# Layer 1 of a sparse graph attention kernel: the owner mask made with ScalarE, owners weighted on ScalarE, score products in smaller pieces

## What is computed

```
h = relu(layernorm(x)); x = x + elu(softmax_adj(leaky_relu(h W a1 + (h W a2)^T)) @ (h W))
h = relu(layernorm(x))
q, k, v = h Wq^T + bq, h Wk^T + bk, h Wv^T + bv
scores  = where(adj > 0, q k^T / sqrt(128), -9e15)
x = x + elu(softmax(scores) @ v)
```

## Time and profile before

| | before |
|---|---|
| median of 3 runs | 1752.17 us (1751.08 to 1753.33) |
| span of the profiled execution | 1752.0 us |
| first and last gather of layer 1 start | 961.48 and 1728.84 us |
| VectorE busy | 1346.6 us (77%), 5825 instructions |
| TensorE busy | 1194.1 us (68%) |
| GpSimd busy | 1175.3 us (67%), 1206 instructions |
| ScalarE busy | 779.5 us (44%) |
| DMA in layer 1 | about 60 GB/s, near 390 GB/s in layer 0 |

### The profile page before, as it was taken

One profiled execution on the slowest core, in us unless ns is written; L12 is line 12 of the kernel. 1 busy time (PEld: TensorE's weight loads), 2 busy tenths in 40 slices (PEclk: granted clock), 3 DMA queues, 4 the chain that ended last, 5 costly groups with the idle time before them and its releaser, 6 DMA issues.

```text
span 1752.0 us, 21963 instructions
## 1 busy us (share of the span) xinstructions
PE 1194.1 (68%) x5314; PEld 931.3 (53%) x5362; DVE 1346.6 (77%) x5825; ACT 779.5 (44%) x1507; POOL 1175.3 (67%) x1206
## 2 busy tenths in 40 slices
PE   2667785867677677776763577677676676766675
PEld 1444453545454455454553566666666666666664
DVE  3468996989888889888896577777767777777776
ACT  2768776877777777877722111111111111111111
POOL 1227775776666676666674777777777777777773
PEclk9778777777777777777755555655656656666665
DMA  9869999999999999999722222222222222222221
GB/s 292 336 245 389 395 396 400 393 391 382 368 381 378 378 393 388 385 376 386 272 64 55 53 56 62 62 60 61 55 60 62 59 62 62 61 62 60 63 62 38
DMA packets 122254, 372.34 MB, mean 213 GB/s; under 512 B 34577, under 2 KB 67858, under 8 KB 89362
## 3 DMA queue, kind: packets, MB, share of 16 engines
q1 hardware_dynamic: 75458, 289.83, 43.1%
q0 software_dynamic: 38464, 81.08, 17.0%
q10 hardware_dynamic: 8208, 0.03, 0.3%
HBM read 358.12 MB, written 12.72 MB: 212 GB/s over the span
## 4 chain that ended last, share of the span: by engine, by line
POOL 35%; DVE 20%; DMA 14%; issue 13%; PE 9%; ACT 5%; SPq 2%; POOLq 0%; ACTq 0%; DVEq 0%
POOL arena L603 34%; DMA table<-arena 12%; ACT arena L1173 4%; PE psum L1412 4%; PE psum L1398 3%; POOL arena L573 2%; DMA arena<-in_adj_dram 1%; DVE arena L759 1%; DVE arena L792 1%; DVE arena L874 1%; DVE arena L867 1%; DVE arena L762 1%; PE psum L1384 1%; DVE arena L883 1%; SPq L446 1%
## 5 line engine op out<-in xcount | busy, mean ns | idle before, releaser
L573 POOL DMA_INDIRECT arena<-table,arena x576 | 553.9, 962 | 266.4 <-issue 159.5
L603 POOL DMA_INDIRECT arena<-table,arena x576 | 593.1, 1030 | 184.0 <-issue 175.2
L1173 ACT ACTIVATE arena<-arena 128x2048 bf16<-128x2048 int32 x256 | 484.9, 1895 | 32.7 <-DMA arena<-in_adj_dram 32.5
L1384 PE MATMUL psum<-arena 128*128 128x18 f32 x768 | 138.7, 312 | 277.2 <-DVE arena L840 277.1
L1351 PE MATMUL psum<-arena 128*128 128x512 bf16 x976 | 291.9, 447 | 24.6 <-ACT arena L1173 20.6
L1384 PEld LDWEIGHTS psum<-arena 128*128 128x128 f32 x768 | 125.2, 242 | 309.5 <-DVE arena L840 309.5
L874 DVE SCALAR_TENSOR_TENSOR arena<-arena 128x131 f32<-128x131 f32 (+1 forms) x768 | 267.7, 349 | 15.4
L1398 PE MATMUL psum<-arena 128*128 128x131 f32 (+1 forms) x768 | 200.9, 433 | 93.5 <-DVE arena L867 93.5
L1398 PEld LDWEIGHTS psum<-arena 128*128 128x128 f32 x768 | 179.3, 329 | 97.2 <-issue 97.2
L1121 DVE TENSOR_TENSOR arena<-arena 128x903 f32<-128x903 f32 x64 | 70.5, 1101 | 177.7 <-DMA arena<-table,arena 177.7
L1351 PEld LDWEIGHTS psum<-arena 128*128 128x128 bf16 x1024 | 117.4, 120 | 164.0 <-issue 84.9
(11 more groups left out here) (199 smaller groups left out, 1993.3 us busy)
## 6 DMA issues: line engine op xcount, KB each, us to landing
arena<-in_adj_dram SPq DMA_DIRECT2D x256, 1024.0 KB, 15.5
arena<-table,arena POOLq DMA_INDIRECT x1152
table<-arena POOLq DMA_DIRECT2D x32, 132.0 KB, 5.0
arena<-table SPq DMA_DIRECT2D x64, 66.0 KB, 15.1
table<-arena SPq DMA_DIRECT2D x16, 256.0 KB, 15.2
arena<-table SPq DMA_DIRECT2D x64, 64.0 KB, 2.1
out_dram<-arena SPq DMA_DIRECT2D x16, 256.0 KB, 2.4
arena<-in_x_dram SPq DMA_DIRECT2D x4, 0.5 KB, 12.3
```

The lines of the kernel that those rows point to most:

```text
L573: pool.indirect_dma_start(Gt[:, v % GROUP, c + 1, :], None, table0, bass.IndirectOffsetOnAxis(idx_now[:, v % GROUP, c:c + 1], 0))\
L603: pool.indirect_dma_start(Gt[:, t % GROUP, c + 1, 0:D], None, table1, bass.IndirectOffsetOnAxis(idx_now[:, t % GROUP, c:c + 1], 0))\
L1173: nc.scalar.activation(mask[:, k, q * QUARTER:(q + 1) * QUARTER], adj_sb[:, k, q, :], ACT.Relu, accum_out=sum_all[:, bass.ds(tile, 1), q:q ...
L1384: last = nc.tensor.matmul(by_slot_ps[k], owned[:, r, c, :], slot_e[:, k, c, :], start=(c == 0), stop=(c == CHUNKS - 1))
```

## The change

`from_end` and the two-step mask are gone. Before the loop VectorE makes three constants: `iota_odd` = 2 x place + 1 (float16), `mid_all` = -(pre + end) and `len_all` = end - pre. ScalarE writes `dist` = |iota_odd + mid| in float16, two buffers, one tile ahead. VectorE makes the mask with one compare, dist < len. The owners are weighted on ScalarE with three activations of 128 columns, right after the exponential, one step earlier than before in the order of the lists; in the place where `weigh` stood VectorE now waits for the first exponential only, ahead of the add-slots. The score products are written in pieces: own slots two at a time (2, 2, 2, 1), owner slots one at a time (3). The sum over them (L1127) is as before.

```
@@ prepare
-                    dve.wait_ge(mine_done, T + t)
-                    nc.vector.tensor_scalar(from_end[:, :], iota16[:, :], end_all[:, at], None, ALU.is_ge).then_inc(fe_done, 1)
...
-                    dve.wait_ge(fe_done, T + t + 1)
-                    nc.vector.scalar_tensor_tensor(out=mine[:, b, :], in0=iota16[:, :], scalar=pre_all[:, at],
-                                                   in1=from_end[:, :], op0=ALU.is_ge, op1=ALU.subtract).then_inc(mine_done, 1)
+                    dve.wait_ge(dist_done, t + 1)
+                    nc.vector.tensor_scalar(mine[:, b, :], dist[:, b % 2, :], len_all[:, at], None, ALU.is_lt)\
+                      .then_inc(mine_done, 1)
@@ score1
-                    nc.vector.tensor_tensor(prod[:, 0:OWN, :], Gt[:, b, 0:OWN, 0:DE],
-                                            u_row[:, b:b + 1, P:].to_broadcast([P, OWN, DE]), ALU.mult).then_inc(e_done, 1)
+                    for c in range(0, OWN, 2):
+                        end = min(c + 2, OWN)
+                        nc.vector.tensor_tensor(prod[:, c:end, :], Gt[:, b, c:end, 0:DE],
+                                                u_row[:, b:b + 1, P:].to_broadcast([P, end - c, DE]), ALU.mult)\
+                          .then_inc(e_done, 1)
                     dve.wait_ge(own_done, u + 1)
-                    nc.vector.tensor_tensor(prod[:, OWN:ROWS, :], Gt[:, b, OWN:ROWS, 0:DE], uq_ps[k], ALU.mult)\
-                      .then_inc(e_done, 1)
-                    dve.wait_ge(e_done, T + 2 * u + 2)
+                    for c in range(CHUNKS):
+                        nc.vector.tensor_tensor(prod[:, OWN + c, :], Gt[:, b, OWN + c, 0:DE], uq_ps[k][:, c, :], ALU.mult)\
+                          .then_inc(e_done, 1)
+                    dve.wait_ge(e_done, T + PRODUCTS * (u + 1))
@@ attend, VectorE
-                        if live(t, 3):
-                            weigh(T + t - 3, m, back)
...
                         if live(t, 3):
+                            dve.wait_ge(p_done, 2 * (T + t - 3) + 1)
                             for c in range(OWN):
@@ before the loop, VectorE
+                nc.vector.tensor_scalar(iota_odd[:, :], iota16[:, :], 2.0, 1.0, ALU.mult, ALU.add).then_inc(spans_done, 1)
+                nc.vector.scalar_tensor_tensor(out=mid_all[:, :], in0=pre_all[:, :], scalar=-1.0, in1=end_all[:, :],
+                                               op0=ALU.mult, op1=ALU.subtract).then_inc(spans_done, 1)
+                nc.vector.tensor_tensor(len_all[:, :], end_all[:, :], pre_all[:, :], ALU.subtract).then_inc(spans_done, 1)
@@ ScalarE
+                def measure_spans(t):
+                    nc.scalar.activation(dist[:, t % 2, :], iota_odd[:, :], ACT.Abs, bias=mid_all[:, t:t + 1]).then_inc(dist_done, 1)
+
+                def weigh_owners(tt, k, r):
+                    act.wait_ge(p_done, 2 * tt + 2)
+                    act.wait_ge(owned_done, tt + 1)
+                    act.wait_ge(acc_done, tt)
+                    for c in range(CHUNKS):
+                        last = nc.scalar.activation(weighted[:, c, :], owned[:, r, c, :], ACT.Identity,
+                                                    scale=p10[:, k, OWN + c:OWN + c + 1])
+                    last.then_inc(weighted_done, 1)
...
+                        if live(t, -1):
+                            if t >= 1:
+                                act.wait_ge(mine_done, T + t)
+                            measure_spans(t + 1)
                         if live(t, 4):
...
                         if live(t, 2):
                             prob_over(T + t - 2, k)
+                            weigh_owners(T + t - 2, k, (b - 2) % GROUP)
```

More of the change, by code:

```diff
@@ L214, in two_layer_graph_attention @@
         accT = place([2, P])
+        iota_odd = place([QCOLS], F16)
+        dist = place([2, QCOLS], F16)
+        mid_all = place([T])
+        len_all = place([T])
         top[0] = common
@@ L347, in two_layer_graph_attention @@
         hot_done = sem("hot_done")
+        spans_done = sem("spans_done")
+        dist_done = sem("dist_done")
         accn_done = sem("accn_done")
@@ L1116, in keep_u @@
                                                    op0=ALU.mult, op1=ALU.add).then_inc(u_kept, 1)
+                PRODUCTS = (OWN + 1) // 2 + CHUNKS
                 def score1(u, b, k, n):
@@ L1155, in attend @@
                             finish(t - 4, T + t - 4, k)
+                nc.vector.tensor_scalar(iota_odd[:, :], iota16[:, :], 2.0, 1.0, ALU.mult, ALU.add).then_inc(spans_done, 1)
+                nc.vector.scalar_tensor_tensor(out=mid_all[:, :], in0=pre_all[:, :], scalar=-1.0, in1=end_all[:, :],
+                                               op0=ALU.mult, op1=ALU.subtract).then_inc(spans_done, 1)
+                nc.vector.tensor_tensor(len_all[:, :], end_all[:, :], pre_all[:, :], ALU.subtract).then_inc(spans_done, 1)
                 nc.vector.tensor_scalar(scaled_bias[:, :], mix_bias[:, 1, :], SCALE, None, ALU.mult).then_inc(dve_consts, 1)
+                dve.wait_ge(spans_done, 3)
                 dve.wait_ge(dve_consts, DVE_CONSTS + 3)
@@ L1296, in _ @@
             with act.Else():
+                def measure_spans(t):
[8 more added lines that the diff above has]
+                    last.then_inc(weighted_done, 1)
+                act.wait_ge(spans_done, 3)
+                measure_spans(0)
                 def attend(g):
```

## The result

The changed kernel takes 1713.39 us (median of 4 runs, 1712.23 to 1716.06) against 1752.75 us before: a ratio of 0.9774, 95% interval 0.976 to 0.9788, or 39.4 us less. 1716 was forecast, with 1709 to 1731 as the range. A second measurement on another chip gave 1714.44 against 1752.53 (0.9782, 0.9766 to 0.9798). The profiled execution took 1712.56 us and spans 1710.8 us, 41.2 less than the span before.

What follows compares the result with a forecast made beforehand. GpSimd's row gathers were taken to bound layer 1. From a profiled span of 1752.0 us, minus 36 for less lengthening, minus 0.2 at the end, plus 0.2 to the median, came 1716 us; range 1709 to 1731.

Steps and rivals of the forecast that it cites:

- The bound: Layer 1: GpSimd's 9 gathers per step set the time, issued without a stop; work taken from VectorE is worth nothing.
- What lengthens a gather: Layer 1 gathers: VectorE instructions with two SBUF sources block them; release 0.81 us before their end; 49.3 us of lengthening.
- The pieces' gaps: Cut score products: a waiting gather slips in between pieces, each holding 0.27 us instead of 0.96; 0.095 us per step.
- rival A: Score products: the pieces hold as one lock of 1.1 us, costing 31 us instead of 6; 1741 us, chance 0.12.
- Add-slots and finish: Six add-slots and two finish instructions on VectorE, 0.14 us held each, met by chance: 0.063 us per step.
- The compare: The mask's new VectorE instruction: takes 0.4 us, costs gathers 0.02 to 0.07 us per step, 0.04 taken.
- Rival B: New lockstep: compare meets GpSimd at the same place every step, costing 13 to 26 us; 1723 to 1736, chance 0.12.
- The sum: Layer 1 gathers: chance meetings leave 0.20 us per step, 13 us of new lengthening, so GpSimd gains 36 us.
- The lockstep: Old mask: GpSimd holds back L1104, so L1110 meets gathers 58 times in 64, 21.9 us; ends with L1110.
- ScalarE and TensorE: Weightings 0.386 us each, distance 0.39 to 0.49; TensorE's sum starts 0.3 to 0.6 us later, hidden by VectorE's waiting.
- rival C: Weightings delay TensorE's sum and VectorE, which becomes the bound; decides from 1.9 us delay per step; 1784 us, chance 0.03.
- The end: After the last gather: pieces add 0.3 us, L867's removal saves 0.5 us; together -0.2 us.

Runs made afterwards that it cites:

- u_psum_2: Changed kernel with score products uncut and u read from PSUM, copied there once per step by VectorE; 1707.00 us, 0.9733 of the kernel before.
- mask_only_2: Kernel before with only the mask changed (ScalarE's distance, one compare), owners and products as before; second run, 1726.42 us, 0.9844 of the kernel before.
- pieces_only_2: Kernel before with only the score products cut in pieces, mask and owners as before; second run, 1717.64 us, 0.9789 of the kernel before.
- owners_only: Kernel before with only the owners' weighting moved to ScalarE; first run, on the slower kind of chip, 1999.5 us against 1982.6 before.

## Why the prediction was right, and where it was not

*The bound.* Right. GpSimd has the same 175 us of pauses and nothing else but its own gathers; time followed lengthening in every kernel on these chips.

*What lengthens a gather.* Right for instructions with two SBUF sources, and no longer only argued: u_psum_2 took away one SBUF source and nothing of the length, and the lengthening beside the product went from 22.5 us (mask_only_2) to nothing. The 0.81 us from release to end hold in every kernel shown. Too narrow in one point: a tensor_scalar with one SBUF source holds gathers as well. The prediction let the compare cost between nothing, "L1104 lengthened none", and 0.41 us. In layer 1 of the kernel before no gather has its point inside L1104, so that row could not tell. Layer 0 of the same trace could: its L789, an instruction of the same form, lengthened eleven gathers, such as that of 378.24, which lasts 1.05 us and ends 0.82 after L789 has ended (378.16 + 0.31).

*The pieces' gaps.* Right: rival A (1741) falls with the gather of 1016.79. The term was 0.095 x 64 = 6.1 us; 40 meetings cost 5.9 us. A piece of 258 columns lasts 0.425 us on average (0.41 estimated), the one of 129 0.285 (0.28).

*Add-slots and finish.* 0.063 x 64 = 4.0 us; the remainder of the 10.5 us beside the pieces is 4.6. The sentence that they might be "missed, as nearly always now" did not come true: the add-slots are met 36 times, at 0.1 us. Some 0.5 us of the 4.6 belong to neither: 11 gathers have their point in the last 0.03 us of `total` (L889), whose other source lies in PSUM, and end 0.84 us after its end. No run says what holds these.

*The compare.* Forecast 0.04 a step, 2.6 us; measured nothing, and this was luck. Rival B's fixed place came, its cost did not: in 22 of the 64 steps a gather has its point 0.17 to 0.18 us into the compare, where it still passes, and from 0.20 us on the three on record were held. Held to the end of the compare, each of the 22 would have lost the remaining 0.24 us, by estimate 5 us in all (0.417 - 0.17 = 0.24, times 22). Its duration was right (0.417 us for 0.4).

*The sum.* 13 us were taken for the new lengthening, 10.5 were left. The median lies 2.6 us below 1716, which looks like the same amount, but the terms don't add up so simply. The forecast means a span of 1752.0 - 36 - 0.2 = 1715.8 us for the profiled execution, and it was 1710.8: 2.9 us from the gathers (38.9 for 36) and 2.75 from the earlier start of the first gather, which was not forecast and isn't an effect of the change, less 0.6 at the end. Against that the median stands 2.6 us above this span, where 0.2 was taken. So part of the closeness is chance.

*The lockstep, the step that was wrong.* The prediction put the 21.9 us of the mask down to L1104 and L1110 alone ("That lockstep ends with L1110") and gave each part its own share. pieces_only_2 shows that the pattern needs the uncut product as well: without it, L1110's counterpart is met 9 times. mask_only_2 shows that the weighing hung on it too. The total was right because every member of the pattern went at once; the split by parts was wrong, by 23 us for the pieces (-36.3, not -13) and by 10 for the mask.

*ScalarE and TensorE.* The three weightings cost 0.391 us each (0.386 taken), but the distance 0.598, above the bound of 0.39 to 0.49. TensorE's sum now waits 100.7 us in all for ScalarE, and VectorE 38.8 us at L867 for TensorE, where it was 7.3. That is rival C's mechanism at 0.6 us a step, against the 1.9 us from which it would decide. The cover held.

*The end.* -0.2 us was forecast, +0.4 came. From the last product to the last sum the changed kernel takes 11.47 us (1690.31 to 1701.78), before 11.62 (1732.05 to 1743.67), so that part is as said; but behind it the next to last finish waits 2.04 us for ScalarE instead of 1.33.

## What to carry to other kernels

When an engine never waits, ask why its instructions last longer than their own minimum: compare the mean with the median and look at what the other engines run at the point where the long ones let go. For indirect gathers issued by GpSimd here, it is VectorE instructions with two SBUF sources, and tensor_scalar even with one. Move the second source to PSUM, or cut long ones, even where that gives VectorE more to do. Before you say that an instruction holds nothing, make sure that some gather has its point late enough inside it. Don't add up shares read from a periodic schedule: one long blocking instruction can set the phase for all that follow, so undo the parts one by one before saying what each is worth.

## What the runs showed of the hardware that was not expected

Cutting one VectorE instruction changed how often two others, which start 7.1 and 8.5 us after it in the step, met a gather: 58 to 9 and 55 to 16 times.

The hold begins sharply. Taking the gathers of the changed kernel whose point lies in the first 0.3 us of a run of pieces, those up to 0.17 us in last 0.94 or 0.95 us (six of them), those from 0.19 us on last 1.12 to 1.19 (five). The 0.14 us of the prediction was a little short. For the float16 mask instruction the limit lies at 0.20 to 0.21 us.

VectorE is held up in its turn. VectorE's copy of nine indices (L1104 in the changed kernel) lasts 0.152 us at the least and up to 0.375 beside a gather, and the float16 mask instruction 0.30 to 0.54 us in the kernel before; the float32 compare from float16 lasts 0.41 to 0.44 us in the changed kernel. The Trainium skill (SBUF — State Buffer, "Who interferes with whom") lists copies and tensor_scalar among what may contend. The traces agree in both directions for tensor_scalar: its float16 form is held back, and it held 91 of the 98 gathers counted above. For the copy they show only the first; it is too short to tell whether it would hold a gather.

The same kernel takes 1752 us on some chips and 1982 us on two others, with layer 0 moving about 340 GB/s instead of 390 and unexplained pauses in layer 1, the longest of 27.4 us on ScalarE in owners_only. On the slower kind, none of the parts tried gained anything; the whole change was not timed there.
